# End of phase 1 in another order, and the first gathers and the first graph layer further back in the queues

## The reference, cut to what matters

```python
xn = layernorm(x)
# graph layer: table row of node n, attention over 4 heads
xt = xn @ weight                                  # 256 columns, 4 heads of 64
alpha = softmax(leaky_relu(al[src[n]] + ar[dst[n]]))
gnn = sum_h alpha[n, h] * xt[dst[n], h]           # the same 64 columns for each head
# linear attention over all nodes (8 heads), then a two-layer block
Q, K = elu(xn @ Wq) + 1, elu(xn @ Wk) + 1
KV, den = K^T (xn @ Wv), Q . sum(K)
m = layernorm(((Q KV) / den) @ Wm) * g1 + b1
y = layernorm(relu(concat(xn, m) @ W1) @ W2) * g2 + b2
x = x + gnn + xn + y
# second layer norm, a shared MLP and the two best of four experts
out = x + shared(layernorm(x)) + gated_experts(layernorm(x))
```

## Time and profile before

| what | value |
|---|---|
| median of 3 runs | 1343.5 us (1343.08 to 1343.95) |
| profiled execution | 1352.19 us |
| its span, first to last instruction | 1350.4 us |
| PE busy | 1312.1 us, 97% of the span |
| DVE busy | 1094.3 us, 81% |
| ACT busy | 733.6 us, 54% |
| POOL busy | 762.7 us, 56% |
| mean granted PE clock | 0.997 |
| chain that ended last, by engine | PE 86%, DVE 4%, issue 3%, ACT 3% |

### The profile page before, as it was taken

How to read it: one execution, slowest core, us unless ns; L and a number is a source line. 1 busy time by engine, 2 the same in 40 slices (tenths; PEclk the granted TensorE clock), 3 DMA queues, 4 the chain that set the end, 5 groups by cost and what they waited for, 6 DMA issues and landing times.

```text
span 1350.4 us, 26301 instructions
## 1 busy us (share of the span) xinstructions
PE 1312.1 (97%) x8812; PEld 1134.8 (84%) x8812; DVE 1094.3 (81%) x2597; ACT 733.6 (54%) x1332; POOL 762.7 (56%) x815
## 2 busy tenths in 40 slices
PE   6999999788999999999999999999999999999998
PEld 6999999676888888888888888888888888888886
DVE  6867677788888888888888888888888888888875
ACT  4555555344646555555646555555645555555654
POOL 5767766735455564656455564656455564656531
PEclk9999999999999999999999999999999999999999
DMA  6787767422121321222121221222121221222000
GB/s 211 250 275 244 245 208 249 135 56 72 35 70 56 78 70 32 68 65 76 36 68 55 78 70 32 68 65 77 36 68 55 78 70 32 70 64 68 26 17 22
DMA packets 65459, 123.23 MB, mean 91 GB/s; under 512 B 31725, under 2 KB 36176, under 8 KB 65422
## 3 DMA queue, kind: packets, MB, share of 16 engines
q1 hardware_dynamic: 57422, 109.25, 25.1%
q0 software_dynamic: 8000, 13.53, 4.6%
HBM read 70.41 MB, written 52.32 MB: 91 GB/s over the span
## 4 chain that ended last, share of the span: by engine, by line
PE 86%; DVE 4%; issue 3%; ACT 3%; POOL 1%; DVEq 1%; POOLq 1%; ACTq 1%
PE psum L255 25%; PE psum L257 25%; PE psum L256 25%; PE psum L467 5%; PE psum L659 1%; PE psum L708 1%; PE psum L699 1%; PE psum L650 1%; ACT scaleT L982 1%; ACTq L1077 1%; PE psum L718 1%; PE psum L542 1%; ACT relu L1075 1%; DVE gnn L1465 1%; POOL ag L1816 0%
## 5 line engine op out<-in xcount | busy, mean ns | idle before, releaser
L1820 POOL TENSOR_TENSOR h_lo<-relu,h_hi 128x1024 fp32r<-128x1024 f32 (+1 forms) x50 | 118.4, 2368 | 148.5 <-ACT h_hi L977 148.4
L255 PE MATMUL psum<-w_hi,h_hi 128*128 128x256 f32 x588 | 166.5, 283 | 1.0 <-ACT e L988 0.8
L257 PE MATMUL psum<-w_hi,h_lo 128*128 128x256 f32 x588 | 166.0, 282 | 0.0
L256 PE MATMUL psum<-w_lo,h_hi 128*128 128x256 f32 x588 | 165.4, 281 | 0.0
L1820 POOL TENSOR_TENSOR s_lo<-relu,s_hi 128x512 fp32r<-128x512 f32 (+1 forms) x45 | 82.7, 1838 | 121.4 <-ACT s_hi L1078 119.8
L255 PE MATMUL psum<-z_hi,w_hi 128*128 128x512 f32 (+1 forms) x300 | 121.6, 405 | 2.4 <-issue 1.1
L255 PE MATMUL psum<-xT_hi,w_hi 128*128 128x512 f32 (+1 forms) x300 | 119.6, 399 | 0.1
L1814 POOL DMA_INDIRECT xg<-table_xt,idx x100 | 99.3, 993 | 35.5 <-issue 31.6
L976 ACT ACTIVATE relu<-psum,h_bias 128x512 f32<-128x512 f32 (+1 forms) x100 | 67.9, 679 | 94.3 <-issue 81.0
L257 PE MATMUL psum<-xT_hi,w_lo 128*128 128x512 f32 (+1 forms) x300 | 117.2, 391 | 0.0
L257 PE MATMUL psum<-z_hi,w_lo 128*128 128x512 f32 (+1 forms) x300 | 117.0, 390 | 0.0
(11 more groups left out here) (274 smaller groups left out, 4291.6 us busy)
## 6 DMA issues: line engine op xcount, KB each, us to landing
xb<-in_x SPq DMA_DIRECT2D x47, 448.0 KB, 3.8
xT_hi_table<-x1T_hi SPq DMA_DIRECT2D x25, 512.0 KB, 2.8
xT_lo_table<-x1T_lo SPq DMA_DIRECT2D x25, 512.0 KB, 3.6
xT_hi<-xT_hi_table SPq DMA_DIRECT2D x25, 512.0 KB
xT_lo<-xT_lo_table SPq DMA_DIRECT2D x25, 512.0 KB
table_xt<-xts SPq DMA_DIRECT2D x24, 455.0 KB, 3.0
out<-xmid SPq DMA_DIRECT2D x24, 448.0 KB
xb<-in_x SPq DMA_DIRECT2D x47, 64.0 KB, 3.8
```

Source lines behind the costliest of these rows:

```text
L255: pe.matmul(out, wh, xh, start=first, stop=False)
L256: pe.matmul(out, wh, xl, start=False, stop=False)
L257: return pe.matmul(out, wl, xh, start=False, stop=last)
L1820: ptt(out, src, hi, ALU.subtract).then_inc(S[done], 1)
```

## The change

On PE, the last groups of phase 1 are written out in another order: keys of group 23, the hidden bias (now into columns of bank 0 that the last group's transposes leave free), the transposes of group 24, the tables of 23 with the products of 22, the keys of group 24, q of group 0 (into banks 0 and 1), the tables of 24 with the products of 23, the products of 24. ACT's and DVE's weight preparation starts one or two groups earlier (ACT behind groups 21, 22 and 23; DVE's small constants behind group 20, its first `w_lo` part behind group 22). The copy of the hidden bias moves into `p1_lowT` of the last group. The four W2 slices of `w_lo` move to the end of DVE's turn0, its last part to the end of turn1. POOL subtracts only the last group's two tiles. The gathers of group 0 go behind the `rstd` of message 0, those of group 1 behind `h_lo` and between the next `rstd`. DVE's softmax and graph layer of group 0 move from before to around `over_den(1)` and `query_low(1)`.

```diff
@@ PE, end of phase 1
-            phase1(NG - 2, (NG - 2) % 2)
-            phase1(NG - 1, (NG - 1) % 2, more=False)
+            v, par = NG - 2, (NG - 2) % 2
+            p1_k(v, par)
             pe.wait_ge(S["w_later"], 16 * LATER_LOADS)
             for o in range(4):
                 for c in range(CK):
-                    last = pe.matmul(psum[:, 0, o:o + 1], wslice(w_raw, "W1", 2 + c, o * P, P), b1_col[:, c:c + 1],
-                                     start=c == 0, stop=c == CK - 1)
+                    last = pe.matmul(psum[:, 0, HB_AT + o:HB_AT + o + 1], wslice(w_raw, "W1", 2 + c, o * P, P),
+                                     b1_col[:, c:c + 1], start=c == 0, stop=c == CK - 1)
             last.then_inc(S["hb_mm"], 1)
+            p1_transpose(NG - 1, 1 - par)
+            for pair in range(2):
+                p1_table(v, par, pair)
+                p1_kx(v - 1, 1 - par, pair)
+            p1_k(NG - 1, 1 - par)
             pe.wait_ge(S["w_lo"], 1)
-            pe.wait_ge(S["kf"], NG)
-            p2_q(0, 0, 2)
+            p2_q(0, 0, 0)
             for pair in range(2):
-                p1_kx(NG - 1, (NG - 1) % 2, pair, last=True)
+                p1_table(NG - 1, 1 - par, pair)
+                p1_kx(v, par, pair)
+            for pair in range(2):
+                p1_kx(NG - 1, 1 - par, pair, last=True)
@@ PE, turn1
                 p2_m(1)
+                pe.wait_ge(S["w2_lo"], 1)
                 pe.wait_ge(S["h_lo"], 2)
@@ ACT, end of phase 1
-            for v in range(NG - 3, NG):
-                phase1(v, v % 2, more=NG - 1 - v)
-                if v == NG - 2:
+            for v in range(NG - 4, NG):
+                phase1(v, v % 2, more=min(2, NG - 1 - v))
+                if v == NG - 3:
                     act.wait_ge(S["w2_mean"], 1)
...
-                if v == NG - 1:
+                if v == NG - 2:
...
-                lo, hi = plain_parts[v - (NG - 3)]
-                act.activation(w_hi[:, lo:hi], w_raw[:, lo:hi], ACT.Copy).then_inc(S["w_hi"], 1)
+                if v < NG - 1:
+                    lo, hi = plain_parts[v - (NG - 4)]
+                    act.activation(w_hi[:, lo:hi], w_raw[:, lo:hi], ACT.Copy).then_inc(S["w_hi"], 1)
@@ ACT, turn0 and turn1
                 message_rows(0)
-                soft_exp(0, True, False)
...
                     if o == 1:
+                        soft_exp(0, True, False)
                         query_high(1)
@@ DVE, p1_lowT
                 dve.wait_ge(S["x1T_hi"], v + 1)
+                if isinstance(v, int) and v == NG - 1:
+                    dve.wait_ge(S["hb_mm"], 1)
+                    dve.tensor_copy(h_bias[:], psum[:, 0, HB_AT:HB_AT + 4])
@@ DVE, end of phase 1
-            for v in range(NG - 3, NG):
-                phase1(v, v % 2, more=NG - 1 - v)
+            for v in range(NG - 5, NG):
+                phase1(v, v % 2, more=min(2, NG - 1 - v))
+                if v == NG - 5:
+                    small_constants()
                 if v == NG - 3:
-                    small_constants()
-                else:
-                    second_parts(v - (NG - 3) - 1)
-            feature_low(0, 2)
+                    second_parts(0)
+            feature_low(0, 0)
+            second_parts(1)
+            feature_high(0, 0)
             dve.wait_ge(S["w_hi"], 3)
...
-            dve.wait_ge(S["hb_mm"], 1)
             dve.memset(kden[:], 0.0)
             dve.wait_ge(S["kx"], NG)
             dve.tensor_copy(kx[:], psum[:, 6:8, 0:KX_W]).then_inc(S["kxs"], 1)
-            feature_high(0, 2)
...
-            dve.tensor_copy(h_bias[:], psum[:, 0, 0:4])
@@ DVE, turn0 and turn1
                 dve.drain().then_inc(S["p1_dve"], 1)
-                soft_chain_in(0, 0, True, False)
+                second_w2(range(4))
...
                 tt(mT_lo[:], colT(0, 2), mT_hi[:], ALU.subtract).then_inc(S["mT"], 1)
+                soft_chain_in(0, 0, True, False)
+                over_den(1, 2)
+                query_low(1)
                 soft_chain_out(0, True, False)
                 graph_layer(0, 0)
-                over_den(1, 2)
-                query_low(1)
-                second_parts(2)
                 message_stats(1)
...
                 soft_chain_out(1, True, False)
+                second_parts(2)
@@ POOL, phase1
-                ptt(xr_lo[par][:, :, 0:C], xn1[par][:], xr_hi[par][:, :, 0:C], ALU.subtract).then_inc(S["x_split"], 1)
+                t = tiles(v)
+                ptt(xr_lo[par][:, 0:t, 0:C], xn1[par][:, 0:t, :], xr_hi[par][:, 0:t, 0:C],
+                    ALU.subtract).then_inc(S["x_split"], 1)
...
-                ptt(k_lo[par][:], kf[par][:], k_hi[par][:], ALU.subtract).then_inc(S["k_split"], 1)
+                ptt(k_lo[par][:, 0:t, :], kf[par][:, 0:t, :], k_hi[par][:, 0:t, :], ALU.subtract).then_inc(S["k_split"], 1)
@@ POOL, turn0 and turn1
             def turn0():
+                rstd(LM, "mv_m", 1, "rs_m")
                 pool.wait_ge(S["tables"], 1)
                 pool.wait_ge(S["idx0"], 2 * dma16(0, 0))
                 gathers(0, range(T))
-                pool.wait_ge(S["idx1"], 2 * dma16(1, 1))
-                gathers(1, (0, 1))
-                pool.drain()
-                rstd(LM, "mv_m", 1, "rs_m")
-                gathers(1, (2, 3))
                 pool.drain()
...
                     low(h_lo[:, 2 * n:2 * n + 2, :], relu[n][:], h_hi[:, 2 * n:2 * n + 2, :], "h_lo")
+                pool.wait_ge(S["idx1"], 2 * dma16(1, 1))
+                gathers(1, (0, 1))
+                pool.drain()
                 pool.wait_ge(S["m_norm"], T)
                 rstd(LM, "mv_m", 2, "rs_m")
+                gathers(1, (2,))
+                pool.drain()
                 rstd(LY, "mv_y", 1, "rs_y")
+                gathers(1, (3,))
+                pool.drain()
                 rstd(LZ, "mv_z", 1, "rs_z")
```

17 lines of the change are left out of this document (10 added, 7 removed), and 2 rows, old and new, of the table SEMAPHORES.

## The result

After takes **1361.41 us** (median of 5 runs, 1360.78 to 1361.82), before 1343.95 (5 runs beside them, 1343.08 to 1347.00): ratio 1.0126, 95% interval 1.0114 to 1.0138. That is 17.5 us slower, where I had forecast 7.1 slower and a range up to 1354.5.

The account below looks back on a forecast made before the run. TensorE bounds the kernel nearly everywhere, so its idles decide; 2.6 + 3.0 + 1.5 = +7.1 us (-1.25 already within the 2.6), added to the median 1343.5, gives 1350.6 us, range 1343 to 1354.5.

Parts of the forecast that it names:

- e: Group 0's gathers behind the first message's rstd: DVE waits before q1's multiply, first message of group 1 +2.6 us.
- f: Group 1's gathers behind h_lo: second message's rstd at P + 7.75 (P: start of group 1's first message), rows +3.0 us.
- g: Last w_lo slice moved to the end of DVE's turn, uncovered before PE's next wait: +1.5 us.
- the clock: PE may fall to its lower clock behind new idles; counted as nothing, with some 3 us of air after P.
- rival B: DVE's remote idles of 2.32 and 3.06 us, beside the twelve gathers, go: 1345.2 us, chance 0.18.
- Steps a to c: End of phase 1: constants earlier, q0 behind the last k, denominators right behind the copy of kx: together -1.25 us.
- Step d: Four W2 slices go behind the first message's statistics on DVE; that message's rstd ends 0.9 us earlier.
- step b: End of phase 1, q0 behind the last k: PE's 1.08 us wait for k_lo is covered, -1.1 us.
- The rule that I weighed: DVE and POOL lock each other out: group 0's graph layer beside h_lo loses 2.4 us, sum up to 0.4 more.
- rival D: Contention of gathers and graph layer with DVE's work is dearer, 2 us each: 1354.6 us, chance 0.1.

Follow-up runs that it names:

- b_shift: The kernel before with only w2_nmean allocated behind h_bias, moving 112 tiles up by 32 bytes: 1348.99 us, ratio 1.0038.
- b_third: The kernel before, unchanged, traced on a chip where it runs at the 1344 us level: 1344.25 us, ratio 1.0003.
- a_align: The kernel after with w2_nmean in the unused half of h_bias's 32 bytes, every tile at its address in before: 1356.33 us, ratio 1.0087.
- seam_only: The kernel before with the diff's order of the seam's three turns, old end of phase 1, old addresses: 1359.97 us against 1353.51, ratio 1.0045.
- p1_align: The kernel after with the seam's turns as in before and every tile at its old address: 1349.32 us, ratio 1.0035.
- soft_late: The kernel after with softmax of group 0 behind over_den(1), query_low(1) and h of group 0: 1357.67 us, ratio 1.0098.
- p1_gath_g: p1_align with group 0's gathers, rstd(0), then group 1's gathers on POOL, last w_lo slice back ahead of second message's statistics: 1349.37 us, ratio 0.9965.
- a_again: The kernel after, unchanged, run again on a chip where before took 1344.38 us: 1361.32 us, ratio 1.0125.
- b_again: The kernel before, unchanged, profiled once more beside itself: 1353.14 us against 1353.31, ratio 0.9999.

## Why the prediction was wrong, point by point

The comparison that isolates the seam is b_shift with after: same addresses, chips of the same kind, 1348.99 and 1361.41 us. Starts on PE from the two timelines, with those of the trace that I had predicted from:

| start on PE, us | trace of before | b_third | b_shift | after | after less b_shift |
|---|---|---|---|---|---|
| first message, group 0 | 273.1 | 267.5 | 268.4 | 266.1 | -2.3 |
| first message, group 1 | 293.4 | 289.1 | 288.8 | 291.9 | +3.1 |
| rows of that message | 301.9 | 297.6 | 297.4 | 305.2 | +7.8 |
| rows of z, group 0 | 314.2 | 309.9 | 309.8 | 319.3 | +9.5 |
| second w2 pair, group 1 | 335.1 | 331.1 | 330.7 | 341.8 | +11.1 |
| scale rows behind it | 338.1 | 336.4 | 333.7 | 346.2 | +12.5 |

The time from one row to the next gives what each term of the sum measured:

| term of the sum | forecast | measured |
|---|---|---|
| e, first message of group 1 | +2.6 | +3.1 |
| f, from there to its rows | +3.0 | +4.7 |
| f, third and fourth tile's gathers, to the rows of z | 0 | +1.7 |
| g, to the second w2 pair | +1.5 | +1.6, by another path |
| the clock, inside that pair | 0 | +1.4 |
| the addresses, all groups | not in the sum | +5.0 |
| sum | +7.1 | +17.5 |

**The steps that failed.** The largest error is a term that I put at nothing without a reason, **the addresses, +5.0**: the diff moves one allocation and I read it as costless. The next is in **step f**: "0.45 + 4.84 us for four gathers and a drain" and "The third and fourth tile's gathers fit before the next two rstd, within 0.1 us" take a gather's issue for its price. The rstd behind it waits for the landing; the rows of the message come 1.7 us later than forecast and those of z another 1.7. (This split is read from the traces; no run takes the landing out.) The address term alone does not explain the miss: a_align, which is without it, takes 1356.33 us and is outside the range too.

**The base of the sum** was unexamined: "It is 8.7 us longer than the median of the runs, 1343.5; I add the difference that I find to the median." The 8.7 us were no even stretch; 5.6 of them are the lag ahead of the first message and some 3.3 the slower groups, and the runs at 1343.5 had neither. It did the forecast no harm, since I had left the idles of the earlier trace rows as they were on both sides. It does rule out rival B against this median: the idles it wanted to win back were not in it. Rival B's guess at the cause is supported by seam_only: on a chip with the lag, with the gathers moved back, those idles are not there. Against the trace of before, after is 9.1 us slower (1361.27 - 1352.19), near my 7.1, but that is luck: two chips are compared, the lag takes 5.6 us off and dearer steps make up for it.

**Steps a to c** (-1.25) were right on PE: k of group 22 starts at 224.15 against 223.09, +1.06 for my +1.0; the denominators start at 257.22 against 258.52, -1.3; the first message of group 0 starts 1.4 us earlier than in b_third. **Step d** (-0.9): the first message's rstd ends at 272.68, against 273.86 in b_third, -1.2, and 274.79 in b_shift, -2.1. But in step b I looked only at what PE gets and not at the last table rows, 4.0 us later, and the gathers behind them. In after nothing waits for the tables there; with the old turns it is part of the 4.9 us of p1_align.

**Step e** (+2.6 at the first message of group 1): +3.1 against b_shift. The gathers ended at 283.23 and landed by 284.8, DVE waited for them ahead of the multiply, PE idled 3.74 us. The mechanism is right. That the size is near is in part luck: from the landing to the multiply it took 2.8 us where I had 1.0, for the subtraction stood beside POOL's h_lo, and the rstd that begins the chain ended 1.2 us earlier than I had it. Against the trace of before it is -1.5, which is the lag again. soft_late shows the wait worth 3.7 us.

**Step f** (+3.0): +4.7 from that message to its rows. The term mis-sized is "0.45 + 4.84 us for four gathers and a drain: the rstd of the second message can start at P + 7.75". It started at P + 9.69: the drain lasts until the gathers have landed, 2.36 us where the sum had next to none. The statistics of DVE were late too, and the rstd itself took 2.9 us instead of 1.9, its first piece 1.19 for 0.20, beside a DVE addition. Both rows of DVE in after:
```profile
298.96 0.25 DVE L1205 BATCH_NORM_AGGREGATE mv_m<-bn_m 128x2 f32<-128x6 f32 x2 [0.18 <-issue]
...
301.51 1.23 DVE L1724 TENSOR_TENSOR base<-base,gnn 128x1024 f32<-128x1024 f32 x1
```
The statistics end at P + 7.3, where I had P + 5.7 at most; without the wait for the landing the rstd could have started there. Behind the third tile's gathers rstd(y) starts at 309.16, 1.80 us behind the gather's end, DVE's xmid waits 1.55 us for it, and z's rows lose another 1.7 us.

**Step g** (+1.5): undoing it was worth 0.8 us in p1_gath_g. In after DVE idles 1.47 us for ACT behind the moved slice of 1.49 us, so the slice was covered. The second w2 pair did start 1.6 us later still, but by another path, DVE beside POOL's h_lo:
```profile
331.48 5.23 DVE L1508 TENSOR_TENSOR s_lo<-relu,s_hi 128x1024 fp32r<-128x1024 f32 x1 [1.47 <-ACT s_hi L987]
```
It takes 1.2 us alone (b_third), and POOL's two h_lo run from 330.85 to 335.61, 1.1 us before it ends. The rule that I weighed from the Trainium skill (SBUF — State Buffer, "SBUF: two separate sides"), the shared port pair as an exclusive lock, is borne out by this row and by the 2.13 us subtraction. The graph layer of group 0, for which I had weighed it, took 4.83 us for twelve steps (2.77 in b_third), and the statistics ended at P + 7.3, inside the P + 7.1 to 8.1 that I had worked out; the rstd stood behind the gathers until P + 9.69 anyway.

**The clock** ("I count nothing"). PE fell to the lower level behind its new idles. In after, behind the 3.74 us, PEclk is 0.65 over 4 us, and the matmuls start 0.21 us apart instead of 0.12 (row 292.30 above, the next starts at 292.51). The 24 matmuls of the message took 4.2 us to 296.15; in b_third 2.8. That 1.4 us cost nothing: PE idles 3.15 us before the rows of the message, and the rstd that ends this idle stood behind the gathers, not behind the message. There the "3 us of air" held. It costs where PE has none, in the second w2 pair, first b_third, then b_shift, then a_again:
```profile
331.06 0.58 PE L255 MATMUL psum<-w_hi,h_hi 128*128 128x256 f32 x1 [3.21 <-ACT e L988]
331.44 0.42 PE L256 MATMUL psum<-w_lo,h_hi 128*128 128x256 f32 x1
331.66 0.42 PE L257 MATMUL psum<-w_hi,h_lo 128*128 128x256 f32 x1
```
```profile
330.71 0.38 PE L255 MATMUL psum<-w_hi,h_hi 128*128 128x256 f32 x1 [2.06 <-ACT e L988]
330.93 0.28 PE L256 MATMUL psum<-w_lo,h_hi 128*128 128x256 f32 x1
331.05 0.28 PE L257 MATMUL psum<-w_hi,h_lo 128*128 128x256 f32 x1
```
```profile
341.88 0.38 PE L256 MATMUL psum<-w_hi,h_hi 128*128 128x256 f32 x1 [3.52 <-ACT e L998]
```
In the first two the pair starts 0.35 us apart and ends 2.7 apart (scale rows at 336.4 and 333.7): this is most of the 2.9 us that the traced execution of b_third took beyond its median. In after the pair costs 4.5 us, 1.4 more than in b_shift. In a_again, the same program, it costs 3.0 (scale rows at 344.9) at the full clock, behind a longer idle, and that execution took 1359.97 us, 1.3 less than the traced one of after. So the clock is some 1.4 us of the 12.4 and differs from execution to execution; no run here kept PE busy in those idles to test it.

**The chances.** The side was right (slower, 0.68), the range was not: its upper end was rival D, one dearer contention, while three terms stood outside it, the addresses, the landing and the clock. The first could be read from the diff, the third from the earlier trace rows; the second only from the indirect DMAs' landings, which I had used in step e and not in step f.

## What to carry to other kernels

Where the traced execution is longer than the runs by more than the effect in question, find out which idles make it so before adding anything to the median; an idle that the change removes may not be in the runs at all. Compare traces only where the kernel before takes the same time on both chips. Diff the addresses as well as the instructions: a small tile that moves to the front of the memory shifts all behind it, and a whole loop of matmuls can slow by half a per cent without a wait that tells of it. An indirect DMA on POOL costs the next work behind a drain, here the rstd, its landing and not its issue.

## What the runs showed of the hardware

- With the operands xT, z and mT 32 bytes beyond a multiple of 64 instead of on one, their matmuls of 512 columns took 1 to 3 ns longer, those with h no longer: 43.43 us a group for 43.23, 1.0038 for the kernel (b_shift); put back in after, 5.0 us less (a_align).
- On two of the chips, PE's semaphore updates come 1 to 5 us late while POOL issues gathers (2.2, 5.2 and 4.8 in b_again), and a steady group takes 43.38 us with 0.1 us of scatter instead of 43.23 with none.
- A drain of POOL ended when the gathers ahead of it had landed: 2.36 us idle behind an issue of 0.94, landing at 301.25, next work at 301.61.
- A two-input subtraction of DVE of 1.2 us took 5.23 beside two of POOL's of 4.76 together, and the first piece of POOL's rstd 1.19 us for 0.20 beside a DVE addition of 1.23.
- The same 24 matmuls ran at the lower clock level throughout behind an idle of 3.21 us (b_third), and at the full one behind idles of 2.06 (b_shift) and 3.52 us (a_again). The length of the idle alone does not decide it.
